# Gated linear attention: later LayerNorm blocks moved to tiles 0 and 1, and a new order of the lead-in

## The chip, the cores and the metric

The kernel runs on one core of one Trainium2 chip. The metric is the time of one execution on the device in microseconds (us). PE is TensorE (its matrix multiplications; PEld its weight loads), DVE is VectorE, ACT is ScalarE, POOL is GpSimd, SP is SyncE.

## What is computed

The program is a stack of eight residual layers over a sequence of 2048 positions (16 tiles of 128) with 128 features: attention, gated linear attention (GLA), a second attention, the same GLA again with the same weights, a Mamba layer, a mixture of experts, a delta-rule layer and the mixture again. The change touches only GLA, which therefore runs twice. Cut from the reference:

```python
x = x + _L0_ffn_ref(_layernorm(x, axis=-1), ...)          # called twice
q1, k1, v = x @ Wq * scale, x @ Wk, x @ Wv                # 8 heads of 64
q2 = (x @ Wqa @ Wqb) * scale
k2 = softmax(x @ Wka @ Wkb)                               # per head
gk1, gk2 = log_sigmoid(x @ Wg_a @ Wg_b + bg) / 16         # two sets of gates
rw = e * one_hot(top_1(e));  e = softmax(x @ We)          # 4 experts
# chunk_gla, chunks of 64:
g = cumsum(gk); qg = q * exp(g); kg = k * exp(-g)
A = tril(qg @ kg.T); o_intra = A @ v                      # scores within a chunk
S = S * exp(g_last) + k_out.T @ v; o_inter = qg @ S       # state over chunks
o = o_dense(q1, k1, v, gk1) + sum_e o_sparse(q2 * rw, k2 * rw, v, gk2 * mask)
o = rms_norm(o) * norm_w * silu(x @ Wga @ Wgb);  return o @ Wo
```

## The kernel before

`gla_ffn` writes one list of instructions for each engine. The lists run freely and meet only at semaphores (`pe.wait_ge(...)`); within an engine the written order is kept, so a waiting instruction holds everything behind it. The 16 tiles t run one after the other; t = 0 .. 15 is the loop `for t in range(NT)` in each of `on_pe`, `on_dve`, `on_act` and `on_pool`. Inside iteration t, PE also makes what tile t+1 needs (and the gate logits of t+2), so each iteration holds the scores, state and output of t beside the preparation of t+1. What stands ahead of the loop is called the lead-in; it prepares tile 0 and part of tile 1.

The k index of many steps is 0 for the dense part and 1 for the expert part. The steps that matter here are:

- `finish_gates(t)` (DVE, L1291) makes the log decays of tile t, after ACT's `gate_magnitude(t)` (L1458) and `softplus(t)` (L1462, L1464) on the logits of `gate_logit(t, k)` (PE, L1013).
- `cumulate(t)` (PE, L1031) sums the decays, and `exp_cumulated(t)` (ACT, L1485 and L1486) exponentiates the sums. `halves(t)` (PE, L1038), `exp_half(t)` (ACT, L1491) and `turn_halves(t)` (PE, L1048) do the same for half chunks.
- `normalise_keys`, `expert_queries`, `decay_keys`, `dense_queries` (DVE, L1306 to L1331) scale keys and queries; `turn_k1`, `turn_q1`, `turn_k0`, `turn_q0` (PE, L1066) transpose them, and ACT copies the results out (L1495 to L1507). `subtract_max` (DVE, L1297 and L1300) and `exp_keys` (ACT, L1479) begin the softmax of the keys.
- `scores(t, k)` (PE, L1097) and `mask_scores(t, k)` (DVE, L1346); `spread_experts` (PE, L1106) and `mask_queries` (DVE, L1353); `gate_project` (PE, L1006), `sigmoid` (ACT, L1448 to L1452) and `weigh_gate` (DVE, L1285) for the output gate; `values` (PE, L1017).
- `inter`, `intra`, `update`, `update_dense` (PE, L1122, L1133, L1140, L1147), then `keys` (L1053), `queries` (L1061), `sum_squares` (L1153), `project` (L1159) on PE. POOL does `decay_state` (L940), `add_scores` (L945), `mask_values` (L933) and `apply_gate` (L950).

The LayerNorm is made in four blocks b of four tiles each: DVE `statistics`, ACT `deviation` (two small instructions a block, L153 and L155), DVE `apply` (four instructions a block, L146), PE `turn` (four transposes, L166), ACT `copy` (L176). Block 0 is made ahead of everything; blocks 1 to 3 are needed only from the end of tile 1 on, where the constant `LATE_BLOCKS` places their low-rank products. `LATE_TURNS = 0` puts their `apply`, `turn` and `copy` in iteration 0.

PSUM has eight banks. `Ring` hands seven of them out in the lead-in in the order of `ENTRY_USES`, and three in the loop in the order of `TILE_USES`; the writer of a bank waits for the reader of the use that stands that many places earlier. `Abank` (banks 3 and 4), `Obank` (5 and 6) and `Dbank` (7) are fixed in the loop. `g.keep_busy(bank, n)` issues n matmuls whose result nobody reads (L74).

## Time and profile before

| | us |
|---|---|
| median of 3 runs (lowest, highest) | 2940.57 (2937.79, 2943.01) |
| the profiled execution, its own time | 2937.7 |
| its span in the profile | 2936.2 |
| first GLA call: first `scores(0, 0)` to the first `cumulate(2)` | 680.50 to 711.46 |
| second GLA call: the same | 1700.33 to 1731.67 |

| engine | busy us over the span | share |
|---|---|---|
| PE | 2742.3 | 93% |
| DVE | 2494.2 | 85% |
| ACT | 2065.0 | 70% |
| POOL | 917.7 | 31% |

Times are counted from the start of the span. Busy shares are means over layers with different limits, so the place of the change has to be read by itself. PE is the engine with most work, but its busy time is modelled, and a matmul at half clock counts as busy too. The granted TensorE clock is given as a share of full speed: 1.00 is 2.4 GHz and 0.50 is 1.2 GHz.

### The profile page before, as it was taken

The page shows a single profiled execution, that of the slowest core. Times are in us where ns is not written, and L with a number is a line of the kernel's source. Part 1 is how long each engine was busy: PE and PEld are TensorE (multiplying, and loading weights), DVE is VectorE, ACT ScalarE, POOL GpSimd, SP SyncE. Part 2 cuts the span into 40 slices and gives each one's busy share as a digit, 9 for nine tenths or more (in the row PEclk, how much of TensorE's full clock was granted, in tenths as well). Part 3 has the DMA queues.
Part 4 walks back from the last instruction along what each step waited for, and adds up shares of the span by engine and source line. Part 5 has one row for each costly group of instructions (what it writes and reads, how often), then busy time and mean ns, then how long its engine had stood idle before and what let it go on. Part 6 is the DMA issues. An engine that isn't in the chain of part 4 may idle for free.

```text
span 2936.2 us, 58135 instructions
## 1 busy us (share of the span) xinstructions
PE 2742.3 (93%) x23139; PEld 1250.7 (43%) x23139; DVE 2494.2 (85%) x3270; ACT 2065.0 (70%) x3906; POOL 917.7 (31%) x1052
## 2 busy tenths in 40 slices
PE   8999999998999989999999989999887799888789
PEld 3222222235666622222222356666333265467655
DVE  8999999987777699999999867776899956899754
ACT  6999999976666579999999766665776423745232
POOL 1000000013444410000000134543477555299810
PEclk8999999999999999999999999999999999989999
DMA  2000000000000010000000000000000000000000
GB/s 96 6 16 17 17 16 17 17 9 1 2 2 2 2 55 11 16 15 17 16 16 14 13 1 2 1 2 28 0 1 0 10 1 1 1 1 1 1 1 15
DMA packets 29148, 33.62 MB, mean 11 GB/s; under 512 B 13195, under 2 KB 23438, under 8 KB 28622
## 3 DMA queue, kind: packets, MB, share of 16 engines
q1 hardware_dynamic: 28878, 29.92, 3.5%
q8 instruction: 182, 2.98, 0.4%
q14 instruction: 88, 0.72, 0.1%
HBM read 17.58 MB, written 7.34 MB: 8 GB/s over the span
## 4 chain that ended last, share of the span: by engine, by line
PE 65%; DVE 20%; ACT 8%; issue 3%; POOL 3%; DMA 0%; SPq 0%; DVEq 0%; POOLq 0%; PEldq 0%; ACTq 0%
PE banks L401 15%; PE banks L383 10%; DVE max_parts L528 7%; PE banks L376 6%; PE banks L2142 2%; PE banks L1122 2%; PE banks L2127 2%; PE banks L1097 2%; PE banks L2129 2%; ACT probs L644 2%; PE banks L1031 2%; DVE banks L2993 2%; DVE state_keys L2990 2%; PE banks L1140 2%; DVE banks L2995 2%
## 5 line engine op out<-in xcount | busy, mean ns | idle before, releaser
L528 DVE TENSOR_REDUCE max_parts<-banks 128x2 f32<-128x1024 f32 x1024 | 1170.6, 1219 | 10.0 <-PE banks L376 8.3
L644 ACT ACTIVATE probs<-banks 128x512 f32<-128x512 f32 x2048 | 1085.4, 600 | 57.7 <-PE banks L383 31.4
L383 PE MATMUL banks<-q_parts,k_parts 51*128 51x512 bf16 x2048 | 653.9, 384 | 4.9 <-ACT v_heads L603 1.5
L401 PE MATMUL banks<-probs,v_heads 128*9 128x256 f32 x8192 | 637.2, 382 | 8.1 <-ACT pv_copy L655 2.0
L376 PE MATMUL banks<-k_parts,q_parts 48*128 48x512 bf16 x2048 | 594.9, 386 | 8.8 <-DVE max_parts L528 5.2
L711 POOL CAST neg_max_parts<-neg_max 128x8 bf16<-128x8 f32 x64 | 12.9, 201 | 1121.4 <-DVE neg_max L533 1121.4
L383 PEld LDWEIGHTS banks<-q_parts,k_parts 51*128 51x128 bf16 x2048 | 151.8, 94 | 473.8 <-ACT probs L644 395.8
L401 PEld LDWEIGHTS banks<-probs,v_heads 128*9 128x9 f32 x8192 | 123.7, 88 | 381.0 <-issue 342.0
L1676 POOL TENSOR_TENSOR state_times_c<-state,c_row 128x1024 f32<-128x1024 f32 x63 | 148.0, 2354 | 90.3 <-ACT c_row L1992 54.4
L1870 DVE TENSOR_TENSOR_SCAN state<-banks,state_carry,state 128x512 f32<-128x512 f32 x128 | 157.3, 1271 | 6.6 <-ACT banks L1987 4.5
L2313 ACT ACTIVATE silu_a<-banks 128x512 f32<-128x512 f32 x80 | 47.7, 597 | 162.8 <-PE banks L2127 162.6
L1754 PE MATMUL banks<-state_times_c,ident 128*128 128x512 f32 x256 | 131.6, 639 | 28.8 <-POOL state_times_c L1676 28.3
L945 POOL TENSOR_TENSOR scores_dense<-scores_dense,scores_expert 128x1024 f32<-128x1024 f32 x32 | 75.5, 2359 | 210.8 <-DVE scores_expert L1346 210.8
L376 PEld LDWEIGHTS banks<-k_parts,q_parts 48*128 48x128 bf16 x2048 | 124.2, 93 | 33.8 <-DVE max_parts L528 19.3
L2209 DVE TENSOR_TENSOR hidden<-silu_a,banks 128x512 f32<-128x512 f32 x80 | 54.8, 688 | 87.9 <-PE banks L2129 82.4
L2914 POOL TENSOR_TENSOR state_decayed<-state,decay 128x512 f32<-128x512 f32 x64 | 109.9, 1717 | 43.1 <-DVE state L2983 31.8
L933 POOL TENSOR_SCALAR v_experts<-v_tile,expert_mask 128x512 f32<-128x512 f32 x120 | 116.7, 990 | 10.1 <-ACT v_tile L1469 10.1
L1987 ACT ACTIVATE banks<-dt,neg_A 128x512 f32<-128x512 f32 x128 | 86.2, 688 | 46.0 <-DVE state L1870 44.4
L2941 PE MATMUL banks<-state_queries,ident 128*128 128x256 f32 (+2 forms) x272 | 75.3, 442 | 38.3 <-POOL state_queries L2920 38.3
L940 POOL TENSOR_TENSOR state_middle<-state_end,state_decay 128x1280 f32<-128x1280 f32 x32 | 74.5, 2329 | 82.9 <-DVE state_decay L1337 82.9
L2142 PEld LDWEIGHTS banks<-ffn_weights,hidden 128*128 128x128 f32 x640 | 85.3, 197 | 30.1 <-issue 22.5
L1485 ACT ACTIVATE exp_cum<-banks 128x512 f32<-128x512 f32 x64 | 38.4, 600 | 81.7 <-PE banks L1031 81.7
(527 smaller groups left out, 5016.8 us busy)
## 6 DMA issues: line engine op xcount, KB each, us to landing
outT_half<-pv_copy SPq DMA_DIRECT2D x248, 16.0 KB
prob_sums<-pv_copy SPq DMA_DIRECT2D x248, 2.0 KB
q_scratch<-qk_parts SPq DMA_DIRECT2D x8, 384.0 KB, 3.5
k_scratch<-qk_parts SPq DMA_DIRECT2D x8, 384.0 KB, 2.6
k_parts<-k_scratch SPq DMA_DIRECT2D x28, 96.0 KB
q_parts<-q_scratch SPq DMA_DIRECT2D x28, 96.0 KB
q_parts<-neg_max_rows SPq DMA_DIRECT2D x128, 3.0 KB
ffn_weights<-moe SPq DMA_DIRECT2D x1, 1928.0 KB, 7.3
```

The costliest lines, as they stand in the source:

```text
L376: nc.tensor.matmul(Mb[m % 2][:, blk(x)], Q[p % 2][half_of(x, ROWS), tile(t)], K[p % 2][half_of(x, ROWS), blk(b)], start=True, stop=True).t ...
L383: nc.tensor.matmul(bank("exp", n, x)[:, :], K[p % 2][half_of(x, ROWS + PARTS), tile(t)], Q[p % 2][half_of(x, ROWS + PARTS), blk(j)], start ...
L401: i = nc.tensor.matmul(PVb[group:group + VD, cols], V[:, t + k, 2 * (s // NB) + x, :], PT[:, (n + k) % RING, x, cols], start=(t == 0 and c ...
L528: nc.vector.tensor_reduce(mxp[s % 2][:, :, u // NB, u % NB], Mb[m % 2].rearrange("p (x k) -> p x k", x=2), AX.X, ALU.max).then_inc(*maxed. ...
L644: nc.scalar.activation(PT[:, n % RING, x, :], bank("exp", n, x)[:, :], ACT.Exp, scale=float(HD) ** -0.5).then_inc(*exped.inc())
L933: i = nc.gpsimd.tensor_scalar(vm[q][:, :, e, :], v_t[q][:, :, :], mask[:, t, e:e + 1], 1.0, ALU.mult, ALU.mult)
L1676: nc.gpsimd.tensor_tensor(G[m % 2][:, :, :], F[m % 3][:, :, :], Cs[m % 2][:, :].unsqueeze(1).broadcast_to([128, 2, 512]), ALU.mult).then_i ...
L1754: nc.tensor.matmul(Yb[c][:, :], g.ident[:, :], G[m % 2][:, c, :], start=(n == 0), stop=(n == NS - 1)).then_inc(*summed.inc())
L1870: nc.vector.tensor_tensor_scan(f, decay_bank(m, c)[:, :], f, carry[:, c, n:n + 1], ALU.mult, ALU.add).then_inc(*scanned.inc())
L1987: nc.scalar.activation(decay_bank(m, c)[:, :], dt[:, c, unit_blk(m)], ACT.Exp, scale=negA[:, c, m % NS:m % NS + 1]).then_inc(*decay_made.i ...
L2142: i = nc.tensor.matmul(Yb(r)[:, tile(c)], hs[:, r % 3, tile(c)], w["w2"][:, u, :], start=(u in first and c == 0), stop=(u in last), skip_g ...
L2914: nc.gpsimd.tensor_tensor(SD[:, :, :, :], S[1 - s % 2][:, :, :, 0:HD], d, ALU.mult).then_inc(*decayed.inc())
```

## The change

It does five things, each in both calls:

1. `LATE_TURNS` becomes a table: block 1 is transposed and copied in iteration 0, blocks 2 and 3 in iteration 1. DVE's `apply` of blocks 1 and 2 moves behind tile 1's preparation in iteration 0 (on either side of `normalise(0)`), that of block 3 to the same place of iteration 1. ACT's `deviation` of the three blocks moves from the lead-in to a place behind `keep_queries(1)` and ahead of `exp_keys(1)`.
2. `cumulate` and `exp_cumulated` are split by k. In the lead-in the cumulations of tile 0 stand ahead of `queries(0)` and of tile 1's gate logits, with `halves(0)` between them (it gets a wait for the decays of its own).
3. ACT's `softplus(1)` moves behind the four copies of tile 0's keys and queries, and DVE's `finish_gates(1)` behind `mask_scores(0, 0)`.
4. `gate_project(0)` and `scores(0, 1)` move on PE from the lead-in and from behind `halves(1)` to a place ahead of `cumulate(1)`; `weigh_gate(0)` moves behind `mask_scores(0, 1)`.
5. Six unread matmuls behind `halves(0)` become two ahead of `cumulate(0, 0)`. `ENTRY_USES` follows the new order.

```diff
@@ -799,10 +799,10 @@
 EARLY, ROUTED_FIRST, ROUTED = 4, 13, 30
 TILE_USES = "cum0 cum1 v rows q2 klow g0 g1 kvd k1 q1 rs tk0 tq0 tk1 tq1 out".split()
 USES_AHEAD = dict(rs=0, out=0, g0=2, g1=2)
-LATE_TURNS, LATE_BLOCKS = 0, 1
+LATE_TURNS, LATE_BLOCKS = {0: (1,), 1: (2, 3)}, 1
 LATE_MASKS = {2: 1, 3: 2, 4: 3}
 ENTRY_USES = (("turned", 0), ("glow", 0), ("low", 0), ("g0", 0), ("g1", 0), ("klow", 0), ("q2", 0), ("mask", 0), ("v", 0), ("same", 0),
-              ("cum0", 0), ("cum1", 0), ("k1", 0), ("q1", 0), ("g0", 1), ("g1", 1), ("gp", 0), ("rows", 0), ("tk1", 0), ("tq1", 0),
+              ("cum0", 0), ("cum1", 0), ("k1", 0), ("q1", 0), ("rows", 0), ("g0", 1), ("g1", 1), ("tk1", 0), ("tq1", 0), ("gp", 0),
               ("tk0", 0), ("tq0", 0))
 
 
@@ -876,8 +876,8 @@
             if t in LATE_MASKS:
                 tile_uses = tile_uses[:-1] + [("mask", LATE_MASKS[t]), tile_uses[-1], ("same", LATE_MASKS[t])]
             uses += tile_uses
-            if t == LATE_TURNS:
-                uses = uses[:-1] + [("turned", b) for b in range(1, NB)] + uses[-1:]
+            if t in LATE_TURNS:
+                uses = uses[:-1] + [("turned", b) for b in LATE_TURNS[t]] + uses[-1:]
             if t == LATE_BLOCKS:
                 uses += [(u, b) for b in range(1, NB) for u in ("glow", "low", "logit")]
         entry = Ring(g.ps[0:7], ENTRY_USES, readers)
@@ -1021,16 +1021,16 @@
                 pe.wait_ge(low_copied, t // 4 + 1)
                 nc.tensor.matmul(bank("klow", t)[:, :], a1T[64:128, tile(t)], w["Wb"][64:128, :], start=True, stop=True).then_inc(*k_low.inc())
 
-            def cumulate(t):
-                for k, lhs in ((0, g.cum[:, :]), (1, cum_s[:, t, :])):
-                    u = f"cum{k}"
-                    pe.wait_ge(gates_made, 2 * t + k + 1)
-                    if k == 1:
-                        pe.wait_ge(same_masked, t // 4 + 1)
-                    pe.wait_ge(*bank_read(u, t))
-                    nc.tensor.matmul(bank(u, t)[:, :], lhs, gk[t % 2][:, k, :], start=True, stop=True).then_inc(*cums_made.inc())
+            def cumulate(t, k):
+                u = f"cum{k}"
+                pe.wait_ge(gates_made, 2 * t + k + 1)
+                if k == 1:
+                    pe.wait_ge(same_masked, t // 4 + 1)
+                pe.wait_ge(*bank_read(u, t))
+                nc.tensor.matmul(bank(u, t)[:, :], (g.cum[:, :], cum_s[:, t, :])[k], gk[t % 2][:, k, :], start=True, stop=True).then_inc(*cums_made.inc())
 
             def halves(t):
+                pe.wait_ge(gates_made, 2 * t + 2)
                 pe.wait_ge(*bank_read("rows", t))
                 pe.wait_ge(masks_begun, 3)
                 for r in range(2):
@@ -1174,15 +1174,15 @@
             values(0)
             same_expert(entry, 0)
             keys(0)
+            g.keep_busy(Dbank, 2)
+            cumulate(0, 0)
+            halves(0)
+            cumulate(0, 1)
+            queries(0)
             gate_logit(1, 0)
             gate_logit(1, 1)
-            queries(0)
-            cumulate(0)
-            halves(0)
-            g.keep_busy(Dbank, 6)
-            gate_project(0)
+            turn_k1(0)
             turn_halves(0)
-            turn_k1(0)
             turn_q1(0)
             turn_k0(0)
             turn_q0(0)
@@ -1190,11 +1190,16 @@
                 after = t + 1 < NT
                 scores(t, 0)
                 spread_experts(t)
+                if t == 0:
+                    gate_project(0)
+                    scores(0, 1)
                 if after:
-                    cumulate(t + 1)
+                    cumulate(t + 1, 0)
+                    cumulate(t + 1, 1)
                     values(t + 1)
                     halves(t + 1)
-                scores(t, 1)
+                if t > 0:
+                    scores(t, 1)
                 if after:
                     low_keys(t + 1)
                     low_queries(t + 1)
@@ -1224,9 +1229,8 @@
                     turn_halves(t + 1)
                     turn_k1(t + 1)
                     turn_q1(t + 1)
-                if t == LATE_TURNS:
-                    for b in range(1, NB):
-                        turn(b)
+                for b in LATE_TURNS[t] if t in LATE_TURNS else ():
+                    turn(b)
                 if t in LATE_MASKS:
                     turn_mask(ring, LATE_MASKS[t])
                 project(t)
@@ -1386,7 +1390,6 @@
             expert_queries(0)
             decay_keys(0)
             dense_queries(0)
-            finish_gates(1)
             dve.wait_ge(zeroed, 2)
             state_decay(0)
             norm.statistics(3)
@@ -1394,12 +1397,11 @@
                 after = t + 1 < NT
                 mask_scores(t, 0)
                 if t == 0:
-                    weigh_gate(0)
+                    finish_gates(1)
                 mask_queries(t)
                 mask_scores(t, 1)
-                if t == LATE_TURNS:
-                    for b in range(1, NB):
-                        norm.apply(b)
+                if t == 0:
+                    weigh_gate(0)
                 if after:
                     subtract_max(t + 1)
                     normalise_keys(t + 1)
@@ -1413,7 +1415,11 @@
                     decay_keys(t + 1)
                     dense_queries(t + 1)
                     weigh_gate(t + 1)
+                if t in (0, 1):
+                    norm.apply(2 * t + 1)
                 normalise(t)
+                if t == 0:
+                    norm.apply(2)
                 if after:
                     state_decay(t + 1)
                 add_x(t)
@@ -1478,12 +1484,11 @@
                 act.wait_ge(k_steps, 7 * t + 2)
                 nc.scalar.activation(kg[t % 2][:, 1, :], kg[t % 2][:, 1, :], ACT.Exp).then_inc(*k_exped.inc())
 
-            def exp_cumulated(t):
-                for k in range(2):
-                    act.wait_ge(cums_made, 2 * t + k + 1)
-                    act.wait_ge(q_dense, t)
-                    nc.scalar.activation(eg[:, k, :], bank(f"cum{k}", t)[:, :], ACT.Exp, scale=1 / 16.0)
-                    nc.scalar.activation(en[:, k, :], bank(f"cum{k}", t)[:, :], ACT.Exp, scale=-1 / 16.0).then_inc(*exp_cums.inc())
+            def exp_cumulated(t, k):
+                act.wait_ge(cums_made, 2 * t + k + 1)
+                act.wait_ge(q_dense, t)
+                nc.scalar.activation(eg[:, k, :], bank(f"cum{k}", t)[:, :], ACT.Exp, scale=1 / 16.0)
+                nc.scalar.activation(en[:, k, :], bank(f"cum{k}", t)[:, :], ACT.Exp, scale=-1 / 16.0).then_inc(*exp_cums.inc())
 
             def exp_half(t):
                 act.wait_ge(halves_made, t + 1)
@@ -1535,24 +1540,28 @@
             copy_values(0)
             keep_queries(0)
             exp_keys(0)
+            exp_cumulated(0, 0)
+            exp_half(0)
+            exp_cumulated(0, 1)
             gate_magnitude(1)
-            exp_cumulated(0)
-            softplus(1)
-            exp_half(0)
             copy_k1T(0)
             copy_q1T(0)
             copy_k0T(0)
             copy_q0T(0)
+            softplus(1)
             sigmoid(0)
-            for b in range(1, NB):
-                norm.deviation(b)
             for t in range(NT):
                 after = t + 1 < NT
                 if after:
-                    exp_cumulated(t + 1)
+                    exp_cumulated(t + 1, 0)
+                    exp_cumulated(t + 1, 1)
                     copy_values(t + 1)
                     exp_half(t + 1)
                     keep_queries(t + 1)
+                if t == 0:
+                    for b in range(1, NB):
+                        norm.deviation(b)
+                if after:
                     exp_keys(t + 1)
                 if t + 2 < NT:
                     gate_magnitude(t + 2)
@@ -1567,9 +1576,8 @@
                     copy_q0T(t + 1)
                     copy_k1T(t + 1)
                     copy_q1T(t + 1)
-                if t == LATE_TURNS:
-                    for b in range(1, NB):
-                        norm.copy(b)
+                for b in LATE_TURNS[t] if t in LATE_TURNS else ():
+                    norm.copy(b)
                 if t == LATE_BLOCKS:
                     for b in range(1, NB):
                         copy_low_gates(b)
```

The rows below are instructions in the order in which an engine has them, first call of GLA; in them `log_decay_141` belongs to tile 0 (and 2), `log_decay_142` to tile 1, and the line numbers of after are up to 8 higher. On ACT, in the lead-in from the exponentials of tile 0's sums on, before:

```order
L1485 ACTIVATE exp_cum<-banks 128x512
L1486 ACTIVATE exp_neg_cum<-banks 128x512
L1485 ACTIVATE exp_cum<-banks 128x512
L1486 ACTIVATE exp_neg_cum<-banks 128x512
L1462 ACTIVATE abs_logit<-abs_logit 128x1024
L1464 ACTIVATE abs_logit<-abs_logit 128x1024
L1491 ACTIVATE exp_half_rows<-banks 128x256
L1495 COPY k_decayedT_137<-banks 128x512
L1499 COPY q_decayedT_135<-banks 128x512
L1503 COPY k_decayedT_137<-banks 128x512
L1507 COPY q_decayedT_135<-banks 128x512
```

And after, from the same place:

```order
L1490 ACTIVATE exp_cum<-banks 128x512
L1491 ACTIVATE exp_neg_cum<-banks 128x512
L1496 ACTIVATE exp_half_rows<-banks 128x256
L1490 ACTIVATE exp_cum<-banks 128x512
L1491 ACTIVATE exp_neg_cum<-banks 128x512
L1464 ACTIVATE abs_logit<-banks 128x512 x2
L1500 COPY k_decayedT_137<-banks 128x512
L1504 COPY q_decayedT_135<-banks 128x512
L1508 COPY k_decayedT_137<-banks 128x512
L1512 COPY q_decayedT_135<-banks 128x512
L1468 ACTIVATE abs_logit<-abs_logit 128x1024
L1470 ACTIVATE abs_logit<-abs_logit 128x1024
```

The two `abs_logit` rows of 1024 columns (`softplus(1)`) stood ahead of `exp_half_rows` and now stand behind the four transposed copies; the read-out of tile 1's logits (128x512 x2) now stands in between.

On PE, at the start of iteration 0 (`scores(0, 0)` is the first row, 1030 is 1031 before):

```order
 L1097 MATMUL banks<-q_decayedT_135,k_decayedT_137 128x128 x8
 L1106 MATMUL banks<-expert_mask_rows,expert_select 128x128 x4
-L1031 MATMUL banks<-log_decay_142,cum 128x512
-L1031 MATMUL banks<-log_decay_142,same_expert_cum 128x512
+L1006 MATMUL banks<-low_rank_gates,ffn_weights 128x128 x4
+L1097 MATMUL banks<-q_decayedT_135,k_decayedT_137 128x128 x8
+L1030 MATMUL banks<-log_decay_142,cum 128x512
+L1030 MATMUL banks<-log_decay_142,same_expert_cum 128x512
```

`gate_project(0)` and the expert half of the scores now stand ahead of tile 1's two cumulations; the scores row has gone from its place a few rows further on.

On DVE, in iteration 0 from `mask_scores(0, 0)` to tile 1's keys, before:

```order
L1346 TENSOR_TENSOR scores_dense<-banks,tri 128x512 x2
L1285 SCALAR_TENSOR_TENSOR out_gateT_125<-banks,ffn_weights,gate_sigmoid 128x512
L1353 TENSOR_TENSOR q_experts<-q_decayedT_135,banks 128x2048
L1346 TENSOR_TENSOR scores_expert<-banks,same_expert_tri 128x512 x2
L146 TENSOR_SCALAR ln_space<-x_tok,ln_space 128x128 x12
L1297 TENSOR_REDUCE k_stats<-banks 128x8
L1300 TENSOR_TENSOR k_decayed_134<-banks,k_stats 128x512
```

After, the same stretch, and then the end of the iteration from `dense_queries(1)` to `state_decay(1)`:

```order
L1350 TENSOR_TENSOR scores_dense<-banks,tri 128x512 x2
L1295 SCALAR_TENSOR_TENSOR log_decay_142<-banks,abs_logit 128x512 x2
L1357 TENSOR_TENSOR q_experts<-q_decayedT_135,banks 128x2048
L1350 TENSOR_TENSOR scores_expert<-banks,same_expert_tri 128x512 x2
L1289 SCALAR_TENSOR_TENSOR out_gateT_125<-banks,ffn_weights,gate_sigmoid 128x512
L1301 TENSOR_REDUCE k_stats<-banks 128x8
L1304 TENSOR_TENSOR k_decayed_134<-banks,k_stats 128x512
```

```order
L1335 SCALAR_TENSOR_TENSOR q_decayed<-banks,exp_cum 128x512
L1289 SCALAR_TENSOR_TENSOR out_gateT_126<-banks,ffn_weights,gate_sigmoid 128x512
L146 TENSOR_SCALAR ln_space<-x_tok,ln_space 128x128 x4
L1373 TENSOR_TENSOR outT_tile<-outT_tile,out_square 128x512
L146 TENSOR_SCALAR ln_space<-x_tok,ln_space 128x128 x4
L1341 TENSOR_TENSOR state_decay<-exp_second_half_139,banks 128x20
L1343 COPY exp_second_half_140<-banks 128x20
```

The twelve normalisations stood between tile 0's masked scores and tile 1's keys. Eight of them now stand around the multiplication `outT_tile` (`normalise(0)`), and the other four have gone to iteration 1; tile 1's decays have come in behind the dense scores.

## Rows read from the trace of the kernel before

**Rows 1.** The head of the page.

```profile
span 2936.2 us, 58135 instructions
```

**Rows 2.** Busy time by stretch: iteration 0 in each call (us, busy, instructions, PEclk, DMA).

```profile
681.99:711.46 29.47, 23.59 (x239) 15.44 (x239) 22.46 (x39) 16.11 (x34) 8.65 (x7) 0.88 0.01 2
...
1701.82:1731.67 29.85, 23.97 (x240) 15.58 (x239) 22.47 (x39) 16.11 (x34) 8.65 (x7) 0.89 0.00 1
```

**Rows 3.** Chain that ended last, lead-in of the first call (start, us, what).

```profile
675.03 0.95 ACT abs_logit L1462
...
676.01 1.06 ACT abs_logit L1464
...
679.86 0.50 ACT q_decayedT L1507
...
680.50 1.16 PE banks L1097 x16
681.66 0.33 PE banks L1106 x4
```

**Rows 4.** The same chain, iterations 0 and 1 of the first call.

```profile
685.36 1.14 PE banks L1097 x16
...
687.77 6.74 DVE ln_space L146 x12
...
696.53 0.70 DVE k_stats L1306
...
700.43 2.07 PE banks L1053 x2
702.51 1.59 PE banks L1061 x2
...
707.59 1.40 PE banks L166 x12
...
716.61 0.88 PE banks L1006 x8
...
724.11 1.05 PE banks L1053 x2
725.17 0.86 PE banks L1061 x2
```

**Rows 5.** PE's timeline, iteration 0 (start, us, instruction, [idle before, releaser]).

```profile
695.89 0.69 PE L1147 MATMUL banks<-v_tile,k_decayed 128*64 128x64 f32 x16 [1.54 <-DVE k_decayed L1300]
700.43 2.07 PE L1053 MATMUL banks<-ffn_weights,xnT 128*128 128x512 f32 x2 [3.86 <-DVE log_decay L1291]
```

**Rows 6.** DVE's timeline, first call of GLA.

```profile
659.02 1.12 DVE L146 TENSOR_SCALAR ln_space<-x_tok,ln_space 128x128 f32<-128x128 f32 x4 [0.60 <-ACT ln_space L155]
...
675.13 0.69 DVE L1315 TENSOR_TENSOR k_decayed<-k_decayed,exp_neg_cum 128x512 f32<-128x512 f32 x1 [1.20 <-ACT exp_neg_cum L1486]
...
677.54 1.28 DVE L1291 SCALAR_TENSOR_TENSOR log_decay<-banks,abs_logit 128x512 f32<-128x512 f32 x2
...
687.68 6.82 DVE L146 TENSOR_SCALAR ln_space<-x_tok,ln_space 128x128 f32<-128x128 f32 x12
...
719.09 0.69 DVE L1306 TENSOR_REDUCE k_stats<-k_decayed 128x8 f32<-128x512 f32 x1 [0.70 <-ACT k_decayed L1479]
...
723.00 1.28 DVE L1291 SCALAR_TENSOR_TENSOR log_decay<-banks,abs_logit 128x512 f32<-128x512 f32 x2
```

**Rows 7.** POOL's timeline, iterations 0 and 1.

```profile
687.85 2.38 POOL L945 TENSOR_TENSOR scores_dense<-scores_dense,scores_expert 128x1024 f32<-128x1024 f32 x1 [6.46 <-DVE scores_expert L1346]
...
729.33 2.33 POOL L940 TENSOR_TENSOR state_middle<-state_end,state_decay 128x1280 f32<-128x1280 f32 x1 [2.77 <-DVE state_decay L1337]
```

**Rows 8.** ACT's timeline: the first of the six deviations.

```profile
682.08 0.28 ACT L153 ACTIVATE ln_space<-ln_space,eps_ln 128x4 f32<-128x4 f32 x1
```

**Rows 9.** Busy time and granted clock in two short stretches, columns as in rows 2.

```profile
679.00:681.00 2.00, 1.07 (x14) 0.87 (x14) 1.16 (x8) 1.97 (x5) 1.94 (x1) 1.00 0.00 0
...
698.00:700.00 2.00, 0.00 (x0) 0.00 (x0) 1.97 (x4) 1.97 (x3) 0.00 (x0) 0.50 0.02 4
```


## Prediction

> **What bounds the kernel now.** The head of the page gives a span of 2936.2 us [rows 1]; the execution itself took 2937.7, which is 2.9 below the median of 2940.57. I make the sum against 2937.7 and move it to the median at the end. The change is inside GLA, which runs twice, so I went to the chain of waits and looked where it leaves PE in a GLA call. In the later iterations the chain hardly leaves PE. It leaves it at two places in the stretch that the change rewrites.
>
> The first is the lead-in: the chain is on ACT from before 675.03 until the first scores can start at 680.50, and 0.95 + 1.06 us of it are `softplus(1)` (L1462, L1464), which serves tile 1, while tile 0's transposed keys wait behind it [rows 3].
>
> The second is iteration 0: behind the scores the chain goes to DVE, stays 6.74 us in the twelve normalisations (L146) and returns to PE at 700.43, with `keys(1)` [rows 4]. PE's timeline shows the same from the waiting side: PE idle 1.54 us ahead of L1147 and 3.86 us ahead of L1053, whose releaser is `finish_gates(2)` (L1291), the last thing in DVE's run of tile 1's keys [rows 5]. The reader is to see also that L1053 then takes 2.07 us, and L1061 1.59, where one iteration later they take 1.05 and 0.86 [rows 4]. While PE stood still the granted clock had fallen to 0.50, which is 1.2 GHz [rows 9]. The whole stretch from `cumulate(1)` to `cumulate(2)` takes 29.47 us in the first call and 29.85 in the second, with PE busy 23.59 and 23.97 of it [rows 2].
>
> **The lead-in.** The dense and the expert exponentials of tile 0 end at 675.03, and there `softplus(1)` starts [rows 3]. Without it 0.95 + 1.06 = 2.01 us leave the chain, if nothing else is late next. What is late next is DVE: from L1315 at 675.13 its four steps on tile 0's keys and queries run until 677.54 [rows 6], 2.41 us. Then come the transposition of the dense keys (a third of the twelve L166, 0.47 [rows 4], with its tail 0.6), two copies of 0.5 (the last one is the row at 679.86 [rows 3]) and 0.14 of issue. That is 677.6 + 0.6 + 1.1 + 0.14 = 679.4 if the exponentials end where they did, a gain of 1.1. But the expert cumulation now stands ahead of `queries(0)`, a matrix product of 0.86 us [rows 4], and the logits of tile 1 are out of the way too, so I take the exponentials 0.9 earlier: first scores at 678.5, a gain of 2.0 (ends 1.1 and 2.0). PE waits for this chain, so the two matmuls of keep-busy instead of six are worth nothing by themselves.
>
> This gain is spent at once. Ahead of `cumulate(1)` PE now has scores 1.16, spread 0.33, `gate_project(0)` 0.88 and `scores(0, 1)` 1.14 [rows 3, 4]: 678.5 + 3.5 = 682.0, and before it began at 681.99 [rows 2]. So at this mark the change is worth 0.0, with a loss of 0.9 at the worse end.
>
> **Iteration 0.** From that mark on I take pieces out of the 29.47 us:
> - `scores(0, 1)`, done already: 1.14 [rows 4].
> - PE's two waits: 1.54 + 3.86 = 5.40 [rows 5].
> - the half clock: 2.07 + 1.59 - 1.05 - 0.86 = 1.75 [rows 4].
> - eight of twelve transposes: two thirds of 1.40 = 0.93 [rows 4].
>
> Together 9.22, which leaves 20.25. I add 0.4 for a wait of `low_keys(1)`: PE arrives there 1.14 earlier than before, and its bank is given free by ACT's copy of v, which isn't earlier (ends 0 and 0.7). So 20.65, 8.8 us saved.
>
> That the waits vanish has to be shown on DVE, since DVE gives up the normalisations but takes in `finish_gates(1)`. Its run of tile 1's keys (L1297 on) started at 687.77 + 6.74 = 694.51 and released PE at 700.43, 5.92 later [rows 4]. Now it can start when `low_keys(1)` is ready: PE starts that at 685.36 + 0.4, plus 1.05 for a product of this size [rows 4], so 686.8. (DVE itself is free earlier: dense scores, decays, queries, expert scores and gate end near 686.1.) With 5.92 the release is at 692.7. Two things lengthen it. The six deviations now stand on ACT ahead of `exp_keys(1)`; the first took 0.28 [rows 8], and six take about 1.3, of which some 0.7 are hidden behind DVE's own L1297 and L1300: 0.6. And the keys now meet POOL's work: from the start of L1306 to the release took 700.43 - 696.53 = 3.90 in iteration 0 [rows 4], but 723.00 - 719.09 + 0.65 = 4.56 in iteration 1 [rows 6]: 0.7. So 694.0. PE reaches `keys(1)` at 700.43 - 5.40 - 1.14 + 0.4 = 694.3. The release is 0.3 ahead. It is a narrow margin, and rival 1 is its loss.
>
> The eight normalisations that stay come after `weigh_gate(1)`. There, four cost 1.12 [rows 6], as block 0's did; on their present place twelve cost 6.82 instead of 3.36 [rows 6], while POOL ran its L945 of 2.38 from 687.85 [rows 7] and the masking of values behind it. At the new place POOL has nothing until DVE's state decay: in iteration 1 it stood idle 2.77 ahead of L940 [rows 7]. Four normalisations push `normalise(0)` by up to 0.6, and PE meanwhile has four transposes of block 1 (0.47) ahead of `project(0)`: covered. The Trainium skill says the same of the port (Advanced Engine Details and Errata, VectorE Performance Modes): VectorE's second SBUF port is shared with GpSimd, so two-port VectorE instructions and GpSimd ones block each other. The measured 1.12 and 6.82 agree with it. By the rule alone, a place beside POOL's work would cost twice as much here too.
>
> **Iteration 1.** It takes in eight transposes, 0.93 on PE, ahead of `project(1)`, and four normalisations on DVE, of which PE's transposes hide most: 1.0 lost, 1.5 at the worse end. The copies by ACT come in idle time ahead of the low-rank products.
>
> **Sum.** First call: 0.0 + 8.8 - 1.0 = 7.8. The second call is the same code and was 0.4 longer in the same stretch [rows 2], nearly all of it in slow products; it should come to the same 20.65: 8.2. Together 16.0: 2937.7 - 16.0 = 2921.7, and against the median 2940.57 - 16.0 = 2924.6. I predict 2924.5, a ratio of 0.9945. A measurement of this kernel can tell 0.2%, 5.9 us, from no change.
>
> **Rival 1: DVE is still late.** The wait ahead of L1053 shrinks but stays. Its price is bounded by the two additions: all six deviations in the path (1.3) and the port met twice as hard (2 x 0.7), less the margin of 0.3, a wait of 2.4 a call. If PE's clock falls again in it, 1.75 more. The gain is then 16.0 - 4.8 = 11.2, or 7.7 with the clock: 2929 to 2933, say 2930. For it: the margin of 0.3 rests on a chain of some fifteen steps. Against: iteration 1 has the same order and shows no wait at all at its L1053 at 724.11. Chance 0.20.
>
> **Rival 2: PE's clock falls in the lead-in (slower).** Four unread matmuls go, and the lead-in now has two gaps near 0.6 and 1.0 us within 3 us, where PE waits for the queries and for the copies. If the clock fell there to 1.2 GHz and stayed through iteration 0, the 16 us of products until `keys(1)` would take up to 16 longer, and the call would lose 8 instead of gaining 8: 2940.57 + 16 = 2957. It decides the sign once about 8 us of products run at half clock in each call. Against: in the present lead-in PE was busy only 1.07 of 2.0 us and the clock stayed 1.00 [rows 9]; it fell only with waits of 1.54 and 3.86 close together [rows 5]. Chance 0.05. The Trainium skill (TensorE: Matmul & The Clock Gate, Part 1) says that the clock follows how busy PE has been lately, and that the default is the slow state. By it, less keep-busy work is a risk; of these two gaps it says nothing that would change the sum.
>
> **Rival 3: nothing to tell.** What PE waits for in iteration 0 is not the normalisations but a step that the change leaves late, such as the state or the masked values on POOL, and the wait reappears there. Then only the lead-in and the transposes move, and the time is within 5.9 of before, say 2938. Against: the chain names L146 itself, and DVE ran without a pause from 687.77 to L1300. Chance 0.07.
>
> **Numbers.** The forecast has 0.68; its own range is 2920 to 2929 (0.9 a call in the lead-in, 0.5 in iteration 1, and the runs' own spread of about 3). To hold 8 in 10 the range takes in rival 1: 2919 to 2932. Faster by over 0.2%: 0.68 + 0.20 = 0.88. Within: 0.07. Slower: 0.05.
>
> **What would show it.** After: first scores about 2.0 earlier than 680.50, counted from the same start of the call, `cumulate(1)` at the same time, `cumulate(2)` 8.8 earlier and the clock at 1.00 throughout; L146 in three groups of about 1.12; no idle time over 0.5 ahead of L1147 and L1053; iteration 1 longer by 1.0. The prediction is wrong if the idle time ahead of L1053 is over 1 us, if a granted clock of 0.50 appears between the lead-in and `cumulate(2)`, or if `cumulate(1)` starts later than before.

## The result and the profile after

| | before | after |
|---|---|---|
| median of 6 runs each, same chip (us) | 2940.39 | 2923.55 |
| lowest, highest | 2937.79, 2943.01 | 2917.82, 2926.89 |
| ratio, 95% interval | | 0.9948 [0.9937, 0.9958] |
| the profiled execution: own time, span | 2937.7, 2936.2 | 2922.78, 2921.4 |

The medians differ by 16.8 us; the ratio of 0.9948 stands for 15.3 (12.3 to 18.5 by its interval). The prediction was 2924.5, a ratio of 0.9945.

The head of the page and the busy times of after:

```profile
span 2921.4 us, 58119 instructions
...
PE 2735.9 (94%) x23131; PEld 1247.4 (43%) x23131; DVE 2485.6 (85%) x3270; ACT 2066.5 (71%) x3906; POOL 920.0 (31%) x1052
```

PE is busy 6.4 less than before (2742.3), DVE 8.6 less (2494.2): less than the time saved. The rest is idle time of PE that has gone.

PE's timeline of after, first call (columns as in [rows 5]):

```profile
657.19 1.07 PE L166 MATMUL banks<-ident,ln_space 128*128 128x128 f32 x4 [0.21 <-DVE ln_space L146]
...
674.67 0.63 PE L1066 MATMUL banks<-ident,k_decayed 128*128 128x128 f32 x4 [0.58 <-DVE q_decayed L1335]
...
676.51 1.16 PE L1097 MATMUL banks<-q_decayedT,k_decayedT 64*128 64x128 f32 x16 [0.77 <-ACT k_decayedT L1508]
...
680.10 1.12 PE L1030 MATMUL banks<-log_decay,cum 128*128 128x512 f32 x2
...
683.86 0.69 PE L1022 MATMUL banks<-ffn_weights,low_rank_qk 64*128 64x512 f32 x1 [0.35 <-ACT v_tile L1475]
...
691.86 0.64 PE L1147 MATMUL banks<-v_tile,k_decayed 128*64 128x64 f32 x16
692.43 1.12 PE L1053 MATMUL banks<-ffn_weights,xnT 128*128 128x512 f32 x2
...
697.28 0.63 PE L1066 MATMUL banks<-ident,q_decayed 128*128 128x128 f32 x4 [0.48 <-ACT k_decayedT L1508]
697.75 0.60 PE L166 MATMUL banks<-ident,ln_space 128*128 128x128 f32 x4
...
700.64 1.08 PE L1030 MATMUL banks<-log_decay,cum 128*128 128x512 f32 x2
...
718.87 1.08 PE L166 MATMUL banks<-ident,ln_space 128*128 128x128 f32 x8
```

Both waits of [rows 5] are gone: L1147 and L1053 follow without a pause, and L1053 takes 1.12 where it took 2.07.

The stretches from `cumulate(1)` to `cumulate(2)` (first and third row) and on to `cumulate(3)` (second row), and one short one, columns as in [rows 2]:

```profile
680.17:700.80 20.63, 19.80 (x216) 13.36 (x216) 16.70 (x33) 15.81 (x33) 8.48 (x7) 1.00 0.01 2
700.80:730.12 29.32, 28.86 (x272) 19.33 (x271) 17.97 (x38) 18.45 (x33) 10.17 (x8) 1.00 0.01 1
1694.49:1715.12 20.63, 19.80 (x215) 13.36 (x216) 16.70 (x33) 15.81 (x33) 8.48 (x7) 1.00 0.00 1
...
692.00:694.00 2.00, 2.00 (x22) 1.21 (x18) 1.96 (x5) 1.67 (x4) 0.22 (x1) 1.00 0.00 0
```

Iteration 0 takes 20.63 in both calls where it took 29.47 and 29.85 [rows 2], and the clock is 1.00. (These stretches begin where the chain has `cumulate`; by PE's timeline above, which the rest of the text uses, it is 680.10 to 700.64, 20.54, against 29.48.) Ahead of `keys(1)`, where PE stood and the clock was 0.50 [rows 9], PE is now busy 2.00 of 2.00.

DVE's and then POOL's timeline of after, in the same iteration:

```profile
683.47 0.74 DVE L1289 SCALAR_TENSOR_TENSOR out_gateT<-banks,ffn_weights,gate_sigmoid 128x512 f32<-128x512 f32 x1
685.02 0.69 DVE L1301 TENSOR_REDUCE k_stats<-banks 128x8 f32<-128x512 f32 x1 [0.81 <-PE banks L1022]
...
687.57 0.69 DVE L1310 TENSOR_REDUCE k_stats<-k_decayed 128x8 f32<-128x512 f32 x1 [1.14 <-ACT k_decayed L1485]
...
688.80 0.69 DVE L1316 TENSOR_TENSOR k_decayed<-k_decayed,k_stats 128x512 f32<-128x512 f32 x1
689.52 0.69 DVE L1319 TENSOR_TENSOR k_decayed<-k_decayed,exp_neg_cum 128x512 f32<-128x512 f32 x1
...
690.74 1.28 DVE L1295 SCALAR_TENSOR_TENSOR log_decay<-banks,abs_logit 128x512 f32<-128x512 f32 x2
...
695.71 1.11 DVE L146 TENSOR_SCALAR ln_space<-x_tok,ln_space 128x128 f32<-128x128 f32 x4
```

```profile
683.63 2.35 POOL L945 TENSOR_TENSOR scores_dense<-scores_dense,scores_expert 128x1024 f32<-128x1024 f32 x1 [6.54 <-DVE scores_expert L1350]
685.96 2.70 POOL L933 TENSOR_SCALAR v_experts<-v_tile,expert_mask 128x512 f32<-128x512 f32 x4
```

The first of the two L1295 ends near 690.74 + 0.65 = 691.4 and releases PE, which comes at 692.43: DVE is 1.0 ahead. It now waits itself, 0.81 for PE and 1.14 for ACT. Each group of four L146 takes 1.1, as in [rows 6] at 659.02.

**A measure inside the call.** Between two executions the layers outside GLA differ by more than the effects that are to be told apart. So I count from the first transposition of block 0 (L166, at 657.19 above; 659.44 and 1679.26 before, 657.19 and 1671.47 after) to marks inside the same call. By PE's timelines, in us, first and second call:

| from the call's start to | before | after |
|---|---|---|
| first scores (L1097) | 21.06, 21.07 | 19.32, 19.36 |
| `cumulate(1)` | 22.38, 22.40 | 22.91, 22.95 |
| `cumulate(2)` | 51.86, 52.24 | 43.45, 43.49 |
| `cumulate(15)`, the last | 333.18, 333.58 | 325.87, 325.90 |

The calls are 7.3 and 7.7 shorter, together 15.0. What the layers between the two calls take, from the last `cumulate(15)` to the next start, is 686.6 before and 688.4 after, with the same code.

### The profile page after: what moved, and what is told of

Read it like the earlier page. It is cut to its first block, busy times and chain, and to the rows that moved or that the text cites. A ratio compares the mean times of both kernels' runs of the same rounds, so it can differ in the third digit from the quotient of the medians.

```text
span 2921.4 us, 58119 instructions
## 1 busy us (share of the span) xinstructions
PE 2735.9 (94%) x23131; PEld 1247.4 (43%) x23131; DVE 2485.6 (85%) x3270; ACT 2066.5 (71%) x3906; POOL 920.0 (31%) x1052
## 4 chain that ended last, share of the span: by engine, by line
PE 65%; DVE 20%; ACT 8%; issue 4%; POOL 2%; DMA 0%; DVEq 0%; SPq 0%; POOLq 0%; PEldq 0%; ACTq 0%
PE banks L401 15%; PE banks L383 10%; DVE max_parts L528 7%; PE banks L376 6%; PE banks L1122 2%; PE banks L2150 2%; PE banks L2135 2%; PE banks L1097 2%; PE banks L2137 2%; ACT probs L644 2%; PE banks L1030 2%; DVE banks L3001 2%; DVE state_keys L2998 2%; PE banks L1140 2%; DVE banks L3003 2%
## 5 line engine op out<-in xcount | busy, mean ns | idle before, releaser
L945 POOL TENSOR_TENSOR scores_dense<-scores_dense,scores_expert 128x1024 f32<-128x1024 f32 x32 | 75.4, 2357 | 208.5 <-DVE scores_expert L1350 208.5
L933 POOL TENSOR_SCALAR v_experts<-v_tile,expert_mask 128x512 f32<-128x512 f32 x120 | 117.0, 993 | 10.1 <-ACT v_tile L1475 10.1
```

The lines of the kernel that those rows point to most:

```text
L933: i = nc.gpsimd.tensor_scalar(vm[q][:, :, e, :], v_t[q][:, :, :], mask[:, t, e:e + 1], 1.0, ALU.mult, ALU.mult)
```

## The experiments

Every kernel ran on the same chip as runs of before. The diffs show the main lines of an edit against the kernel that is named; "..." stands for what is left out. Medians of before: 2937.88 (13 runs) for the first four kernels, 2938.78 (9 runs) for the last three. Four kernels have one run each; a single time can't tell effects of 1 us a call, so they are judged by their marks, which are the same within 0.04 in both calls of each.

**Norms only.** The lead-in is that of before; deviations, normalisations, transpositions and copies of blocks 1 to 3 are placed as in after. Against before:

```diff
-LATE_TURNS, LATE_BLOCKS = 0, 1
+LATE_TURNS, LATE_BLOCKS = {0: (1,), 1: (2, 3)}, 1
...
-                if t == LATE_TURNS:
-                    for b in range(1, NB):
-                        norm.apply(b)
...
+                if t in (0, 1):
+                    norm.apply(2 * t + 1)
                 normalise(t)
+                if t == 0:
+                    norm.apply(2)
```

> The lead-in of before, the LayerNorm blocks (deviations, normalisations, transposes, copies) placed as after the change. Mark: from a call's first transpose of block 0 to the cumulations; before 22.6 us to cumulate(1) and 52.0 to cumulate(2), after 23.0 and 43.6. My theory: the twelve normalisations ahead of tile 1's keys were what PE waited for, so nearly all of the gain is here: cumulate(1) at 22.6, iteration 0 = 29.5 less the two waits (5.4), the half clock (1.75) and eight transposes (0.9) = 21.4, cumulate(2) at 44.0, iteration 1 longer by 1.0; in all 7.1 per call, 14.2 for the kernel, 2926. Rival (both parts are needed: with DVE still holding the old order, its chain of tile 1's keys stays late): a wait of 1.5 to 2.5 us stays ahead of keys(1), the clock falls again, gain 3 to 4 per call, 2933.

Measured: 2924.82 (4 runs), ratio 0.9953 [0.9936, 0.9969]. First call: `cumulate(1)` at 22.37, as before, and `cumulate(2)` at 44.32, 7.5 earlier. PE's timeline of this kernel, the two waits of iteration 0 that after doesn't have:

```profile
694.03 1.13 PE L1053 MATMUL banks<-ffn_weights,xnT 128*128 128x512 f32 x2 [0.28 <-DVE log_decay L1290]
...
696.25 1.10 PE L1153 MATMUL banks<-out_square,head_ones 128*128 128x512 f32 x2 [0.23 <-DVE state_end L1363]
```

In the second call iteration 0 is the same (21.95 in both), but the clock fell in the lead-in and cost 1.7 (last section). So 3.86 becomes 0.28 by the LayerNorm steps alone (deviations, normalisations and transpositions moved together; the next kernels separate them). The theory held in its mechanism, and that both parts are needed fell. In size it was 0.5 too good: iteration 0 is 21.95 and not 21.4, which is those two waits, and the calls are 6.5 and, with the 1.7, 5.2 shorter by the marks, not 7.1 each.

**Lead-in only.** After, with the LayerNorm steps back where before has them. Against after:

```diff
                 mask_scores(t, 1)
                 if t == 0:
                     weigh_gate(0)
+                if t == LATE_TURNS:
+                    for b in range(1, NB):
+                        norm.apply(b)
```

> The lead-in of after, the LayerNorm blocks as before (twelve normalisations between tile 0's masked scores and tile 1's keys, deviations at the end of the lead-in). My theory: the lead-in's 1.7 us are spent ahead of cumulate(1) (the mark at 23.0, or up to 1 later since the deviations stand ahead of its exponentials), and only what DVE is earlier with the normalisations comes out: keys(1) is released 1 to 1.7 earlier than before, waits of 4 to 5 us and the half clock stay in iteration 0, cumulate(2) at 50.3 to 51.3. Gain 0.7 to 1.7 per call, 1.4 to 3.4 in all, 2937 to 2939, not to be told from no change. Rival (the lead-in is half of the gain): cumulate(2) at 48, gain 4 per call, 2932.

Measured: 2935.37 (10 runs), ratio 0.9992 [0.9981, 1.0003]: by the runs not told apart from no change. By the marks `cumulate(2)` is at 49.84 in the first call and 49.02 in the second, 2.0 and 3.2 earlier than before. PE's timeline of this kernel at the same wait of both calls, and windows around it (columns as in [rows 2]):

```profile
699.12 2.07 PE L1053 MATMUL banks<-ffn_weights,xnT 128*128 128x512 f32 x2 [3.01 <-DVE log_decay L1296]
...
1720.98 1.13 PE L1053 MATMUL banks<-ffn_weights,xnT 128*128 128x512 f32 x2 [3.01 <-DVE log_decay L1296]
```

```profile
700.00:702.00 2.00, 2.00 (x4) 0.83 (x3) 1.88 (x4) 1.31 (x4) 0.58 (x1) 0.50 0.00 0
...
1720.00:1722.00 2.00, 1.02 (x3) 0.54 (x4) 2.00 (x4) 1.94 (x5) 0.00 (x0) 1.00 0.00 0
```

A wait of 3.01 stays of before's 1.54 and 3.86: the lead-in part doesn't remove it, though it takes more off than the theory had (4 to 5 were to stay). After the same wait the clock was 0.50 in the first call and 1.00 in the second, which is the difference of 0.8 between the two calls. Both marks lie between the theory's range and the rival's 48, so neither number held; the first call's is 0.5 ahead of the range, and the twelve normalisations took 6.39 here, not the 6.82 of before.

The two parts overlap: 7.5 and 2.0 alone, 8.4 together. Both take from the same wait, and the normalisations alone already remove nearly all of it.

**Deviations early.** After, with the six deviations back at the end of the lead-in:

```diff
             sigmoid(0)
+            for b in range(1, NB):
+                norm.deviation(b)
             for t in range(NT):
...
                     keep_queries(t + 1)
-                if t == 0:
-                    for b in range(1, NB):
-                        norm.deviation(b)
```

> After, with the six deviations back at the end of the lead-in on ACT (as before the change). Theory from after's timeline: at their new place they lie in a wait of DVE that had 1.0 us to spare before keys(1), so they cost nothing there; at the old place they hold up tile 1's exponentials and behind them ACT's copy of v, for which low_keys(1) waits: that wait grows from 0.35 to about 1.4, iteration 0 from 20.6 to 21.7, cumulate(2) at 44.7 instead of 43.6. Rival (my prediction's reading: at the new place they lengthen the keys' chain by 0.6 at a margin of 0.3): cumulate(2) 0.3 to 0.6 earlier, at 43.0 to 43.3.

Measured, one run: 2923.55 (span 2922.3). `cumulate(2)` at 44.39, 0.94 later than in after. ACT's timeline of this kernel:

```profile
682.68 0.28 ACT L153 ACTIVATE ln_space<-ln_space,eps_ln 128x4 f32<-128x4 f32 x1
...
683.95 0.58 ACT L1490 ACTIVATE exp_cum<-banks 128x512 f32<-128x512 f32 x1
```

The six deviations fill 682.68 to 683.95 and hold tile 1's exponentials; behind these PE waits 0.40 ahead of L1038 and 0.81 ahead of L1022, 1.21 in place of after's 0.35. That is the 0.9. Their new place in the keys costs no time on the path. The theory held, and the prediction's worry fell: it read the deviations as a cost of the change, and their move is a gain of 0.9 a call.

**Block 1 at its old place.** As the kernel before this, and block 1's four normalisations (a third of the twelve) back ahead of tile 1's keys:

```diff
                 if t == 0:
                     weigh_gate(0)
+                if t == 0:
+                    norm.apply(1)
```

> As e3_deviations_early, with the four normalisations of block 1 back behind weigh_gate(0) on DVE, where POOL adds the scores and masks the values. Theory (VectorE's two-port instructions and POOL's shut each other out): the four take 3.5 to 4.5 us instead of 1.1, and since DVE waits there for only 1 to 2 us, tile 1's keys start 1.5 to 2.5 later than in e3_deviations_early; PE waits ahead of keys(1) for 0.5 to 1.5, cumulate(2) that much later. Rival (the twelve took 6.8 because of what they are, not of where they stand): four take 1.1 to 2.3 and vanish in DVE's wait, cumulate(2) as in e3_deviations_early.

Measured, one run: 2923.09 (span 2921.6). DVE's and POOL's timelines of this kernel:

```profile
683.65 3.94 DVE L146 TENSOR_SCALAR ln_space<-x_tok,ln_space 128x128 f32<-128x128 f32 x4
687.50 0.68 DVE L1301 TENSOR_REDUCE k_stats<-banks 128x8 f32<-128x512 f32 x1
```

```profile
683.15 2.35 POOL L945 TENSOR_TENSOR scores_dense<-scores_dense,scores_expert 128x1024 f32<-128x1024 f32 x1 [6.54 <-DVE scores_expert L1350]
685.48 2.70 POOL L933 TENSOR_SCALAR v_experts<-v_tile,expert_mask 128x512 f32<-128x512 f32 x4
```

Four normalisations that take 1.11 alone take 3.94 here, and end near 687.5, while POOL is busy until 688.2. Seen from the call's start, DVE's L1301 comes 2.0 later than without them (30.78 against 28.77), PE waits 0.56 ahead of L1053 and 0.29 ahead of L1153, and `cumulate(2)` is at 45.56, 1.17 later. So the place beside POOL costs more than the work: the theory held.

The single instructions show how (number of them: shortest, median and longest in ns; first and last start). L146 in iteration 0 of before, and then of this kernel:

```profile
L146 DVE TENSOR_SCALAR ln_space<-x_tok,ln_space x12: 333/336/2375, 687.7 to 694.2; 128x128 f32<-128x128 f32 x12
```

```profile
L146 DVE TENSOR_SCALAR ln_space<-x_tok,ln_space x4: 746/754/1939, 683.6 to 686.8; 128x128 f32<-128x128 f32 x4
```

Where POOL is idle, each takes 0.34. Of before's twelve, the second lasts 2.38, as long as POOL's L945 (687.85 to 690.23), the next four about 0.75 each, while POOL's four L933 take 0.69 each, and from 692.9 on, where POOL has ended, the last six take 0.33 to 0.34 again, at the same place in DVE's order. Here the first lasts 1.94 and ends with L945 near 685.5, and the other three take 0.75 beside the L933. So DVE's instruction isn't slowed in proportion; it lasts about as long as POOL's. The price depends on what POOL has to do there more than on how many normalisations stand there: that is why a third of the twelve still costs 3.94 of the 6.82. The prediction's "twice as much" beside POOL was the mean over these twelve, of which only five were held up. The Trainium skill (Advanced Engine Details and Errata, VectorE Performance Modes) has the shared SBUF port, at which VectorE's two-port instructions and GpSimd's block each other, as the reason, and gives no factor. These durations agree with it; the port itself no row shows.

**Expert scores back.** After, with `scores(0, 1)` behind `halves(1)` again:

```diff
                 if t == 0:
                     gate_project(0)
-                    scores(0, 1)
...
-                if t > 0:
-                    scores(t, 1)
+                scores(t, 1)
```

> After, with scores(0, 1) back behind halves(1) as in every other iteration. Theory of the prediction (the lead-in's gain is spent ahead of cumulate(1) on work that has then been done): cumulate(1) 1.1 to 1.2 earlier, at 21.7 to 21.8, iteration 0 longer by 0.7 to 1.1 (the scores come back in, the wait of 0.35 ahead of low_keys(1) is filled by them), cumulate(2) at 43.1 to 43.5. Rival (the early expert scores are what frees DVE's chain of tile 1's keys): cumulate(1) is earlier too, but keys(1) waits for DVE by 0.5 to 1.0, cumulate(2) at 44.0 to 44.5.

Measured, one run: 2927.87 (span 2926.4). `cumulate(1)` at 22.43, 0.5 earlier than in after, where 1.1 was expected: PE waits 0.53 for tile 1's decays. `cumulate(2)` is at 44.27, 0.8 later than in after, which is the rival's number. DVE's timeline of this kernel:

```profile
685.08 1.29 DVE L1348 TENSOR_TENSOR scores_expert<-banks,same_expert_tri 128x512 f32<-128x512 f32 x2 [1.80 <-PE banks L1097]
...
690.27 1.08 DVE L1314 TENSOR_TENSOR k_decayed<-k_decayed,k_stats 128x512 f32<-128x512 f32 x1
691.39 1.07 DVE L1317 TENSOR_TENSOR k_decayed<-k_decayed,exp_neg_cum 128x512 f32<-128x512 f32 x1
```

DVE stands 1.80 for the late scores, POOL's work moves back with them (L933 from 688.78 on, for 3.14), and now two of DVE's products run beside it: 1.08 and 1.07 where after has 0.69 each. PE waits 0.30 and 0.23 behind that. The account closes: 1.09 of scores, 0.53 of new waits (0.30 and 0.23), less the 0.35 that vanishes ahead of L1022, is 1.3, and iteration 0 is 21.84 against 20.54. My theory, that the move only shifts 1.14 of work, fell.

**No keep-busy.** After without the two unread matmuls of the lead-in:

```diff
-            g.keep_busy(Dbank, 2)
             cumulate(0, 0)
```

> After, without the two unread matmuls ahead of cumulate(0, 0), so with none in the lead-in behind block 0's products. Theory: PE waits there for tile 0's decays anyway, so the marks stay: first scores at 19.3, cumulate(1) at 22.9, cumulate(2) at 43.5, and the granted clock stays 1.00 from there to cumulate(2). Rival 2 of the prediction (less keep-busy work lets PE's clock fall in the lead-in): a granted clock of 0.50 ahead of or in iteration 0, and cumulate(2) later by 1.5 to 16.

Measured, one run: 2924.93 (span 2923.5). The marks are 19.32, 22.92, 43.45 and 325.91, those of after within 0.04; PE is idle 0.44 where the two matmuls stood, and no matmul of the stretch is slow in either call. Nothing here speaks for rival 2.

**Squares before queries.** What is left in all of after's iterations is a wait of 0.46 to 0.48 ahead of the last transposes (697.28 above). Here `sum_squares` goes ahead of `queries(t+1)` and the transposes that need the queries go last; the order of the banks follows:

```diff
                     keys(t + 1)
-                    queries(t + 1)
...
                 sum_squares(t)
+                if after:
+                    queries(t + 1)
...
                     turn_k0(t + 1)
-                    turn_q0(t + 1)
-                    turn_halves(t + 1)
                     turn_k1(t + 1)
+                    turn_q0(t + 1)
                     turn_q1(t + 1)
+                    turn_halves(t + 1)
```

> After, with sum_squares(t) ahead of queries(t + 1) on PE, turn_k1 ahead of turn_q0, turn_halves last, the banks and ACT's copies in the same order. It is meant for the wait of 0.46 to 0.48 that stands once in each iteration ahead of turn_q1, whose bank is free only after rms and the copy of the dense keys on ACT. Theory: the squares are ready in time (ACT idles 1.9 us ahead of the root), the root and the copies come 0.8 earlier, the wait goes; a late iteration takes 20.2 instead of 20.64, 15 iterations in two calls save 13, 2910. Rival: turn_q0 then waits for dense_queries on DVE, or sum_squares for the squares, by the same 0.4: iteration 20.6, no change.

Measured: 2914.87 (5 runs), ratio to before 0.9922 [0.9906, 0.9939]. A late iteration of this kernel:

```profile
792.91:813.33 20.42, 20.31 (x229) 13.60 (x227) 15.86 (x27) 13.49 (x24) 10.09 (x8) 1.00 0.01 2
```

It is 20.42 against 20.64 in after: a saving of 0.22, half of the wait, less than expected. The other half comes back ahead of the squares, as the rival had it in part: `sum_squares` (L1153) starts at 806.89, 1.23 behind `keys` (L1053), right when ACT's squares (L1524, 806.21 + 0.63) are done, where `queries` in that place starts 0.96 behind in after (693.39 - 692.43). Iteration 0 is 0.58 longer (21.12 against 20.54). It waits 0.20 for the squares and 0.27 for `normalise(0)`, which stands behind the four normalisations of block 1. A whole call is 322.8 to `cumulate(15)` against 325.9 in after, and 10.4 and 10.8 shorter than before's two: 21.2 together, which would be a ratio of 0.9928. It is faster than before; against after the marks say 6.2 us, and the two intervals just touch.

## Why the prediction was right

| step of the prediction | predicted | measured |
|---|---|---|
| first scores earlier | 2.0 | 1.7 |
| `cumulate(1)` earlier | 0.0 | -0.5 |
| iteration 0 | 20.65 | 20.63 (20.54 by PE's timeline) |
| `cumulate(2)` earlier, first and second call | 8.8, 9.2 | 8.4, 8.8 |
| iteration 1 longer | 1.0 | 1.0 |
| both calls together | 16.0 | 15.0 |

**The lead-in.** The sum was 0.5 too good by PE's timeline, and 0.4 by the chain (`cumulate(1)` at 680.17), from which the prediction had taken this mark. Nearly all of it is in two places. The first scores came 1.7 earlier, not 2.0: the 0.14 of issue between DVE's last row and the transposition was left out, and DVE's steps took 0.1 more than the 2.41. And `gate_project(0)` took 1.08 (678.00 to 679.09 in after's chain), not the 0.88 of a later iteration in [rows 4]. By its own last sentence the prediction counts as wrong where `cumulate(1)` starts later than before; it does, by 0.5. So one of its three signs came true. The size is inside the bound of 0.9 that was given, and what failed with it is the price of the steps ahead of `cumulate(1)`, not their order. These 0.5 in each call are the 1.0 between 16.0 and 15.0.

**Iteration 0.** The pieces came as listed: no wait at L1147 and L1053, no half clock, eight transposes fewer, the scores done before. The new wait of `low_keys(1)` is 0.35, for the 0.4 taken. "Norms only" shows that the waits of 1.54 and 3.86, and the half clock behind them, come of the LayerNorm steps; "block 1 at its old place" shows that a third of the normalisations in that place is enough to bring a wait of 0.56 back.

**The margin.** Predicted 0.3, measured 1.0, and this is the step that was read wrong in part. From the start of tile 1's keys on DVE to the release it took 691.4 - 685.0 = 6.4, not 5.92 + 0.6 + 0.7 = 7.2. The deviations cost 0.45 (DVE waits 1.14 ahead of L1310, and 0.70 in "deviations early") for the 0.6 taken. The 0.7 for POOL didn't come: POOL's L933 ended at 688.66 and DVE's L1316 began at 688.80. In "expert scores back" POOL is later, and the two products (1.08 and 1.07, where after has 0.69 each) take 0.77 longer together. So the size was right and its condition was not: it falls due only if POOL starts late, and `scores(0, 1)`, which the change has moved ahead, lets POOL start early. The prediction had counted this move as 1.14 of work done sooner, which alone gains nothing over the whole call. It is worth 0.8 a call.

**Iteration 1.** 29.32 against 28.33 in before's second call: 1.0 for eight transposes and four normalisations, as predicted.

**The rivals.** Rival 1 (DVE still late) is what "expert scores back" (a wait of 0.30 ahead of L1053, by POOL's late work) and "block 1 at its old place" (0.56) make: the mechanism is real, but after is 1.0 away from it. Its price was too high in the prediction: 0.6 of the deviations' 1.3 and 0.7 of the port's 1.4 were already in the release at 694.0 that gave the margin, so by the prediction's own numbers the wait was at most 1.3 + 1.4 - 0.6 - 0.7 - 0.3 = 1.1 a call and not 2.4, which without the clock is about 2927 and inside its own range of 2920 to 2929. Rival 2 (the clock falls in the lead-in) didn't occur in after's two calls, nor in the two without any keep-busy. That it can't occur isn't shown: in the second call of "norms only", with the lead-in of before, the clock did fall in the lead-in, without a wait. So the prediction's argument against it (it fell only with two waits close together) doesn't hold, though the fall cost 1.7 there and not 16. Rival 3 fell with "norms only".

**The whole.** The medians differ by 16.8 and the marks by 15.0. The 1.8 between them lies inside the interval. The stretch between the calls took 686.6 to 691.3 in the eight profiles in which its code is the same (all but "squares before queries"), so a few us of a single profile say nothing.

## What to carry to other kernels

Where engines keep a written order, look for work that nobody needs soon standing ahead of work that another engine waits for; move it to a place where its engine has time, and price it there, not at its old place. For DVE's normalisations beside POOL, look at the durations of the single instructions: here they lasted as long as POOL's instruction beside them, so one in a bad place cost up to 2.4 us, and one behind it 0.34. Before pricing a moved step by its own duration, follow what it feeds: here the early scores were worth more through POOL's earlier end than through their own time. Count marks from a start inside the same stretch: where the clock stayed, they repeated to 0.04 us here, while whole executions differ by several us.

## What the runs showed of the hardware

**The granted clock.** The same 3.01 of waiting, with the same instructions around it, left the clock at 0.50 in one call and at 1.00 in the other ("lead-in only"). And it fell where PE had no wait at all: in the second call of "norms only", whose lead-in is that of before. Its windows, columns as in [rows 2]:

```profile
1680.00:1682.00 2.00, 2.00 (x11) 1.12 (x11) 1.01 (x3) 1.97 (x3) 0.00 (x0) 1.00 0.00 0
1682.00:1684.00 2.00, 2.00 (x6) 1.02 (x6) 2.00 (x4) 2.00 (x5) 1.73 (x3) 0.82 0.00 0
1684.00:1686.00 2.00, 2.00 (x4) 0.67 (x2) 1.90 (x5) 0.25 (x1) 1.51 (x3) 0.50 0.00 0
```

PE is busy 2.00 of 2.00 in each such window from 1674 on, and yet the clock goes to 0.50; `queries(0)` (L1061) takes 2.08 there. The first scores came at 22.76 instead of 21.04, 1.7 lost that no wait explains. After's profile has a slow stretch as well, outside GLA, ahead of the Mamba layer: 0.50 from 2035 to 2037, and there PE had been idle for half of the two microseconds before. The Trainium skill (TensorE: Matmul & The Clock Gate, Part 1) ties the clock to how busy PE has been lately; a PE busy by the trace (its busy time is modelled) was no guard here, and why the clock fell in this call and not in the first stays open.

**VectorE beside GpSimd.** Four normalisations of 128x128 from SBUF to SBUF took 1.11 alone and 3.94 beside POOL's work: single ones 0.34 alone, 0.75 beside POOL's L933 of 0.69, and 2.38 beside its L945 of 2.38. A product of 128x512 with both inputs in SBUF (L1316) took 0.69 alone and 1.08 beside L933, and one of the L933 took 1.13 there instead of 0.70. A reduction from SBUF (L1310, 687.57 above) took 0.69 beside L933 as it did alone. So the penalty isn't one factor: it is a wait for the other engine's instruction, and not all instructions have it.
